# Decoder block on one core: another order of the projection, the root, the turned rows and the turned biases around the end of self-attention

## The reference, cut to what matters

```python
x = layernorm(x + gated_linear_attention(x))
x = layernorm(x + cross_attention(x, ctx, indices))
x = layernorm(x + block(x))                       # 16 heads of 16, 8 experts of 256 -> 1024 -> 256

def block(x):                                     # the part that the change touches
    h = ln(x, g1, b1)
    q, k, v = h @ Wq + bq, h @ Wk + bk, h @ Wv + bv
    attn = softmax(where(causal, q @ k.T / 4, -inf))
    a  = (attn @ v) @ Wo + bo + x
    h2 = ln(a, g2, b2)
    logits = h2 @ Wr + br
    w  = softmax over the two largest logits
    mid = gelu(h2 @ e_w1 + e_b1);  eo = mid @ e_w2 + e_b2
    return sum(w * eo over the experts) + a
```

## Time and profile before

| | us |
|---|---|
| median of 3 runs | 1402.24 (1400.15 to 1402.31) |
| the profiled execution | 1402.5 |
| its span | 1400.8 |
| TensorE busy with matmuls in it | 1304.1 (93%) |
| VectorE, ScalarE, GpSimd busy | 977.7, 646.7, 138.0 |
| last group's TensorE work of the change | 618.81 to 642.80 |
| first matmul of the experts | 644.97 |

### The profile page before, as it was taken

The page is one execution under the profiler, slowest core; times in us unless marked ns, Lnnn a source line. Parts: engine busy times, 40 slices in busy tenths (PEclk is TensorE's granted clock), DMA queues, the critical chain, the costliest instruction groups (busy, mean ns, idle before and its releaser), DMA issues.

```text
span 1400.8 us, 18778 instructions
## 1 busy us (share of the span) xinstructions
PE 1304.1 (93%) x7483; PEld 960.1 (69%) x7483; DVE 977.7 (70%) x1409; ACT 646.7 (46%) x946; POOL 138.0 (10%) x217
## 2 busy tenths in 40 slices
PE   8787768999889999999999999999999999999997
PEld 6353437656655555456787888888888888888886
DVE  6998986788688788865756656555555556555566
ACT  5697564436457777785324233322323323233233
POOL 5000002000512333211000000000000000000000
PEclk9998879999999999999999999999999999999999
DMA  4000001001642122202000012110201102010001
GB/s 136 1 1 0 0 1 35 0 1 66 191 103 58 49 66 55 68 31 83 24 16 16 1 31 75 38 46 16 68 15 38 46 11 72 16 38 16 0 16 46
DMA packets 38599, 55.76 MB, mean 40 GB/s; under 512 B 8976, under 2 KB 23744, under 8 KB 38512
## 3 DMA queue, kind: packets, MB, share of 16 engines
q1 hardware_dynamic: 33328, 43.67, 10.7%
q0 software_dynamic: 3648, 10.09, 2.6%
q10 hardware_dynamic: 1536, 0.81, 0.2%
HBM read 43.73 MB, written 10.55 MB: 39 GB/s over the span
## 4 chain that ended last, share of the span: by engine, by line
PE 50%; DVE 3%; ACT 1%; issue 0%; DMA 0%; ACTq 0%; DVEq 0%
PE PS L2444 24%; PE PS L2457 23%; PE PS L122 1%; PE PS L114 0%; DMA x_raw<-L_ffn_e_w 0%; PE PS L2470 0%; PE PS L2230 0%; DVE OT_all L2601 0%; DVE r_st L2284 0%; DVE r_on L2301 0%; DVE x_mid L2594 0%; DVE x_mid L2592 0%; DVE r_on L2281 0%; PE PS L2482 0%; PE PS L2208 0%
## 5 line engine op out<-in xcount | busy, mean ns | idle before, releaser
L2444 PE MATMUL PS<-x_h,x_w 128*128 128x512 f32 x1536 | 400.9, 396 | 0.6 <-ACT x_bias L2529 0.3
L2527 ACT ACTIVATE x_g<-PS,x_bias 128x512 f32<-128x512 f32 x256 | 175.7, 687 | 486.6 <-PE PS L2444 486.5
L2457 PE MATMUL PS<-x_mid,x_w 128*128 128x512 f32 x1488 | 383.8, 393 | 0.0
L2444 PEld LDWEIGHTS PS<-x_h,x_w 128*128 128x128 f32 x1536 | 286.9, 188 | 66.1 <-ACT x_g L2527 1.0
L2457 PEld LDWEIGHTS PS<-x_mid,x_w 128*128 128x128 f32 x1488 | 279.5, 188 | 64.2
L2592 DVE CAST x_mid<-x_g 128x512 fp32r<-128x512 f32 x256 | 109.2, 426 | 270.6 <-ACT x_g L2527 270.5
L2070 DVE TENSOR_REDUCE a_M<-PS 128x2 f32<-128x1024 f32 (+1 forms) x144 | 170.7, 1221 | 30.8 <-PE PS L1780 25.0
L2594 DVE TENSOR_TENSOR x_mid<-x_g,x_mid 128x512 fp32r<-128x512 f32 x256 | 177.3, 693 | 8.8
L2008 ACT ACTIVATE f_parts<-PS 128x512 f32<-128x512 f32 x224 | 121.1, 600 | 39.5 <-PE PS L1834 32.7
L1857 PE MATMUL PS<-f_parts,aV 128*32 128x256 f32 (+1 forms) x960 | 74.2, 390 | 0.0
L695 ACT ACTIVATE c_hot<-c_idxT,c_cid 128x1024 bf16<-128x1024 bf16 x65 | 70.2, 1136 | 7.7 <-PE PS L335 7.7
(11 more groups left out here) (371 smaller groups left out, 1615.5 us busy)
## 6 DMA issues: line engine op xcount, KB each, us to landing
x_raw<-L_ffn_e_w SPq DMA_DIRECT2D x32, 512.0 KB, 3.7
qk_parts<-f_parts SPq DMA_DIRECT2D x16, 512.0 KB, 4.2
x_wb<-route_w POOLq DMA_DIRECT2D x31, 256.0 KB, 3.5
aK<-qk_parts SPq DMA_DIRECT2D x96, 64.0 KB, 2.6
aQ<-qk_parts SPq DMA_DIRECT2D x96, 64.0 KB, 2.5
X<-x SPq DMA_DIRECT2D x4, 512.0 KB, 7.5
out<-X SPq DMA_DIRECT2D x3, 512.0 KB, 2.9
O<-itok_BxSx SPq DMA_DIRECT2D x2, 256.0 KB, 8.1
```

Of the source, the lines that this page charges most:

```text
L2444: last = e.matmul(PS[:, f % 2, :], w1[n % 2][u][:, kt, f * P:(f + 1) * P], self.rows(v, k)[:, kt, :], start=m == 0 and kt == 0, stop=m == ...
L2457: last = e.matmul(PS[:, 2 + 2 * (it % 2) + d, :], w2[n % 2][v][:, f, d * P:(d + 1) * P], mid[u][:, f % RM, :], start=f == 0 and m == 0, st ...
L2527: e.activation(g[s % RG][:, :], PS[:, f % 2, :], ACT.Gelu, bias=b1[:, n, f:f + 1]).then_inc(A.sem, 1)
```

## The change

In `attend`, for TensorE: the projection is issued in two pieces, the row tiles 0 and 1 before scores 5 and the tiles 2 and 3 behind them. From there the sums of quad k - 3 stand before the scores of quad k, for k = 6 and 7. Sums 5 and 6 come before `turn_normed`. Scores 8 follow it, then sums 7, and `logits` behind these. The two warm pairs before the projection and before `turn_normed` are gone; one pair stands between sums 8 and 9, another behind sums 9. For ScalarE, `deviation` stands behind the exponentials of quad 6. In `moe` the biases are turned into bank 6 (RB[0]), and TensorE no longer waits for their copy.

```diff
                 quad_scores(4)
                 quad_sums(NG - 1, 2)
-                warm(2, SPARE)
-                self.project(e, 0, FREE)
-                for k in range(5, 8):
+                self.project(e, 0, FREE, range(2))
+                quad_scores(5)
+                self.project(e, 0, FREE, range(2, TB))
+                for k in range(6, 8):
+                    quad_sums(NG - 1, k - 3)
                     quad_scores(k)
-                    quad_sums(NG - 1, k - 2)
-                warm(2, SPARE)
+                quad_sums(NG - 1, 5)
+                quad_sums(NG - 1, 6)
                 self.turn_normed(e, 0, FREE)
-                quad_sums(NG - 1, 6)
                 quad_scores(8)
+                quad_sums(NG - 1, 7)
                 self.logits(e, 0, FREE)
-                quad_sums(NG - 1, 7)
                 quad_scores(9)
                 quad_sums(NG - 1, 8)
+                warm(2, SPARE)
                 quad_sums(NG - 1, 9)
+                warm(2, SPARE)
...
                 last_exps(5)
+                last_exps(6)
                 self.deviation(e, 0)
-                last_exps(6)
                 last_exps(7)
...
-    def project(self, e, m, rb):
-        e.wait_ge(self.VR.sem, self.VR.at("onT0", m))
-        e.wait_ge(self.AR.sem, self.AR.at("onT1", m))
-        self.token_major(e, self.onT, self.Wo, rb).then_inc(self.SR.sem, 1)
+    def project(self, e, m, rb, ts=range(TB)):
+        if 0 in ts:
+            e.wait_ge(self.VR.sem, self.VR.at("onT0", m))
+            e.wait_ge(self.AR.sem, self.AR.at("onT1", m))
+        last = self.token_major(e, self.onT, self.Wo, rb, ts)
+        if TB - 1 in ts:
+            last.then_inc(self.SR.sem, 1)
...
-                e.transpose(PS[:, 0, 0:E * (NF + KD)], self.eb[:, :], self.ident[0:E * (NF + KD), 0:E * (NF + KD)]).then_inc(SM.sem, 1)
-                e.wait_ge(A.sem, A.at("b1"))
+                e.transpose(PS[:, RB[0], 0:E * (NF + KD)], self.eb[:, :], self.ident[0:E * (NF + KD), 0:E * (NF + KD)]).then_inc(SM.sem, 1)
...
-                e.activation(bias[:, :], PS[:, 0, 0:E * (NF + KD)], ACT.Copy).then_inc(A.sem, 1)
+                e.activation(bias[:, :], PS[:, RB[0], 0:E * (NF + KD)], ACT.Copy).then_inc(A.sem, 1)
```

## The result

| | before | after |
|---|---|---|
| median of 20 runs, us | 1400.16 (1397.60 to 1404.56) | 1396.41 (1393.13 to 1400.24) |
| ratio, 95% interval | | 0.9972 (0.9964 to 0.9981) |
| profiled execution's span, us | 1400.8 | 1396.7 |

The change makes the kernel 3.75 us faster by the medians (1400.16 - 1396.41), 2.7 to 5.0 by the interval. The forecast was 4.7 us less and 1397.5 us. The median of before itself fell from 1402.24 (3 runs) to 1400.16 (20 runs), 2.08 us. That the forecast time is only 1.1 us above the measured one is in part luck: it started from the higher median, and the forecast gain is 0.95 us above the measured one.

A forecast was written before the change was run, and what follows sets the result against it. The prediction took the order of work in the last group, with no engine full, as what costs; 0.87 + 2.57 + 1.00 + 0.3 = 4.7 us gave 1397.5 us, range 1395.8 to 1400.7.

The forecast's parts named there:

- Term one: Split projection and later root in the last group: exponentials 7 end at 631.65 instead of 632.52, 0.87 us won.
- Term two: From the end of exponentials 7 to the logits: 1.76 us instead of 4.33, 2.57 us won.
- Term three: Sums 7 stand before the logits instead of between logits and scores 9: 1.00 us won.
- The last pair: Warm pair behind sums 9 at the block's end: hidden by 0.1 us; uncovered, at the low clock, it would cost 0.4.
- Second: The part on the root a quad later: it comes 1.09 us later, waiting for ScalarE and not for VectorE.
- Term four: Start of the experts: of a gelu 1.1 us earlier, 0.3 us stays, between bounds 0 and 1.1.
- A: Rival: one stretch of low TensorE clock in 626 to 636 cuts the gain to 3.0 us, 1399.2; chance 0.17.
- The pairs taken away at 630 us: By the skill's clock rule, removing the two warm pairs there speaks against the change; the forecast took full clock throughout.
- B: Rival: the whole early gelu stays because expert 1's loads land early enough; gain 5.5 us, 1396.7; chance 0.10.
- C: Rival: a wait missing from the sum is exposed, scores 6 and turn_normed late; gain 1.5 us, 1400.7; chance 0.11.
- D: Rival: without the pair before turn_normed the low clock stays until the block's end; slower, 1404.2; chance 0.04.
- The Trainium skill's rule: About 2.66 us per table switch on ScalarE would shrink the gain to about 2.3 us; given no chance of its own.

The follow-up runs named there:

- e5: The changed kernel run again, nothing edited; median 1395.48 us against 1399.74 for the kernel before, ratio 0.9969.
- e6: The changed kernel with the projection in one piece ahead of scores 5; median 1395.24 us against 1399.74 for the kernel before, ratio 0.9961.
- e9: The kernel before with only the root moved behind exponentials 6; median 1397.46 us against 1399.89 for the kernel before, ratio 0.9984.
- e4: The changed kernel with the root put back ahead of exponentials 6; median 1398.90 us against 1399.88 for the kernel before, ratio 0.9988.
- e7: The changed kernel with sums 6 back behind turn_normed and sums 7 behind logits; median 1397.33 us against 1399.74 for the kernel before, ratio 0.9978.
- e1: The kernel before with only the biases turned in bank 6, without the wait; median 1398.67 us against 1399.88 for the kernel before, ratio 0.9988.
- e2: The kernel before with only the two warm pairs around the last sums added; median 1399.45 us against 1399.88, ratio 0.9993.
- e3: The changed kernel without the two warm pairs around the last sums; median 1394.72 us against 1399.88 for the kernel before, ratio 0.9965.
- e8: The changed kernel with logits and scores 9 ahead of sums 7, one warm pair fewer; median 1396.03 us against 1399.74 for the kernel before, ratio 0.9973.
- e10: The changed kernel with logits and scores 9 ahead of sums 7, one warm pair moved before turn_normed; median 1396.14 us against 1399.89 for the kernel before, ratio 0.9979.
- e11: The changed kernel with the last split of expert 1 one step later on ScalarE and VectorE; median 1396.35 us against 1399.89 for the kernel before, ratio 0.9969.

## Why the prediction was right, and where it was not

**The sum.** The forecast of 4.7 us faster lies inside the interval of the measured 3.75. The traces won 5.09 (784.30 - 779.21) and, in e5, 4.43 (784.30 - 779.87). They are two draws of the last load of expert 1, set against a third, the late one of before.

**Term one, 0.87 forecast, 0.56 measured.** Exponentials 7 end at t 16.02 before and 15.46 after. Exponentials 6 start at 8.42 where I had 8.11, because each piece of the projection takes 1.93 us (619.80 to 621.73, 622.39 to 624.32) and not half of 3.54, 1.77. Together that is 0.32 us. The cut alone costs 0.21 of it: the whole projection takes 3.65 us in e6, where no warm pair stands ahead of it either, and 3.54 in before, behind the pair.

**Term two, 2.57 forecast, 2.56 measured.** From the end of exponentials 7 to logits: 4.33 before, 634.72 - 632.95 = 1.77 after. **Term three, 1.00 forecast, 1.00 measured**: 2.88 between logits and scores 9 before, 1.88 after. From there to the end of the block nothing moved: 4.12 at scores 9, 4.12 at sums_out, 4.09 at the turned biases. The last pair is hidden up to 0.03 us.

**Which edit did it** is where my account was wrong. I booked 2.57 us under `turn_normed` behind three quads' sums, 1.00 under sums 7 and only the 0.87 under the projection and the root. The root's move alone brings 3.25 of 4.12 (e9), undoing it takes 3.39 (e4); the split brings 0.11 (e6) and sums 6 and 7 bring 0.29 (e7). The step that failed is in "Second": I took the root a quad later as a cost of 1.09 us that is hidden, and did not say that it frees exponentials 6, and with them scores 7 and sums 5, from standing behind two table loads. These were the queue before `turn_normed`. I had read the 2.02 us of idle time before scores 7 rightly, and did not carry it into the sum. Nor did I give the clock that stays up, some 1.3 us by the estimate at e9, to the root; it stood under "term two".

The 4.12 us at sums_out come out of the runs as 3.25 for the root (before to e9), 0.58 for the split and the front pairs gone (e9 to e7: 23.12 - 22.54, there already at `turn_normed`, 14.35 - 13.77) and 0.29 for the order of the sums (e7 to after). The split is 0.11 of the 0.58; the rest, 0.47, fits the 0.57 of the pair ahead of the projection, which no run took out alone.

That the split would be nearly neutral I could have read off my own working, which lost 1.4 of its 2.3 us at once: scores 6 stand behind the second piece and sums 3 either way.

**Term four, 0.3 forecast, 0.24 and 0.1 measured** where the buffer of the last load comes free: 40.54 before, 36.18 and 36.32 in the two traces of the changed kernel, less the 4.12 of the group. At the stretch it reads 0.94 and 0.34 (5.06 and 4.46, less 4.12), but 0.70 and 0.25 of that are the last load, which took 5.68 us in the one trace of before and 4.98 and 5.43 in these. The first gelu is 1.1 us earlier as forecast: t 32.78 to 27.52, 5.26, of which 4.12 came with the block. That this is lost again before the last load is issued shows in e1 and e2, where nothing of 0.47 and 1.10 us is left; in e3 0.70 of 1.10 is. The size is near the forecast, but a few tenths are within what the earlier loads move by themselves (0.14 us between the two equal traces).

**The rivals.** A, a low stretch in the group, did not come in either trace of the changed kernel, but came in e8 and e10, whose code is the same up to scores 8 (but for one pair in e10); so it was near. The pairs taken away at 630 us cost nothing, and the two added hold the clock (e3). B did not come: the 0.94 us in the first trace are mostly the late load of before. C: no missing wait was found; my times for `turn_normed` (t 13.55 forecast, 13.78 measured) and logits (16.91 forecast, 17.23 measured) carry only the 0.3 of term one. D is out.

**The Trainium skill's rule** on the cost of a switch of the table set ("ScalarE: Activation LUTs", section "What ACT_TABLE_LOAD costs"), about 2.66 us each, does not fit here: after shows load, root and load in 630.89 - 627.99 = 2.90 us again, so the row was the one to follow.

## What to carry to other kernels

Before weighing a reordering, ask for each late instruction what stands before it on the other engine's queue: here two table loads ahead of four exponentials set TensorE's whole order, and exchanging two lines was worth more than the rest of the change. Count in one clock that starts at a common instruction ahead of the change: with 6 us of movement before it, one trace read this way told 0.1 us apart where twelve runs told 1.5. That holds only up to the first thing that waits for a load: behind it one trace moved by more than the edit under test. Where a start is paced by loads, an earlier start can be lost whole (e1, e2), and moving what depends on the load is the better edit (e11).

## What the runs showed of the hardware that was not expected

- The low clock of TensorE comes at the same place of a kernel: in the four traces with the root ahead of exponentials 6 (before, e1, e2, e4) it falls at t 14.3 to 14.4 and rises at 17.7 to 17.9, although t = 0 lies anywhere from 612.69 to 618.50 us.
- The listed busy time did not tell e8, where the clock fell during the logits, from after, where it held: 3.66 and 3.71 us of the 3.92 ahead of the fall.
- A table load can run ahead of what its own activation waits for: in e4 the load ended 2.03 us before the root started. In before the load ahead of the first gelu did not, and stood idle 1.18 us until the matmuls were there. The gelu has two waits in the code and the root one; that this makes the difference is not shown.
- From the free buffer to the split that needs the 512 KB load it took 4.11 to 5.87 us at the same place of fourteen traces. Two equal traces of the changed kernel differ there by 0.45 us, and by nothing over 0.02 us before the first gelu.
